# Expert rows scaled out of PSUM and added to the tokens' rows in memory by the scatters

## What is computed

```python
x = x + _L0_gnn_ref(_layernorm(x), ...)
x = x + _L0_ffn_ref(_layernorm(x), gate_w, gate_b, w1, w2, w3)
x = x + _L1_gnn_ref(_layernorm(x), ...)
...
probs = softmax(x @ gate_w + gate_b)          # 16 experts
top_probs, top_idx = top_k(probs, 2)          # two experts for each token
top_probs = top_probs / sum(top_probs)        # the gate weights
hidden = silu(x @ w1[e]) * (x @ w2[e])        # 256 -> 512, for the two experts e
out = sum over the two e of top_prob[e] * (hidden @ w3[e])
```

## Times and profile before

| | before |
|---|---|
| runs (3) | 2224.04, 2223.59, 2216.57 us |
| median | 2223.59 us |
| the profiled execution | 2217.96 us |
| its span, first to last instruction | 2215.9 us |
| mean granted TensorE clock | 0.762 |
| PE busy | 1600.6 us (72%) |
| DVE busy | 1663.4 us (75%) |
| ACT busy | 1051.1 us (47%) |
| POOL busy | 1259.5 us (57%) |

### The profile page before, as it was taken

One profiled execution on the slowest core, in us unless ns is written; L12 is line 12 of the kernel. 1 busy time (PEld: TensorE's weight loads), 2 busy tenths in 40 slices (PEclk: granted clock), 3 DMA queues, 4 the chain that ended last, 5 costly groups with the idle time before them and its releaser, 6 DMA issues. The chain is left out here.

```text
span 2215.9 us, 33302 instructions
## 1 busy us (share of the span) xinstructions
PE 1600.6 (72%) x9301; PEld 1139.8 (51%) x9301; DVE 1663.4 (75%) x4230; ACT 1051.1 (47%) x2994; POOL 1259.5 (57%) x1217
## 2 busy tenths in 40 slices
PE   0477677776767766389999994477777777777198
PEld 0477344444544445289999993333333333334176
DVE  8998777777888767587878836688888888887601
ACT  0276254444444424212222224588888888874231
POOL 0288577777777750135666650277777777760042
PEclk9888776667575655599999996776777666768589
DMA  3012465455554452388999985277777777770432
GB/s 114 1 5 10 117 190 134 133 133 134 134 133 133 130 88 69 108 275 274 307 300 305 305 277 164 99 213 208 209 209 209 210 208 204 212 175 4 108 90 24
DMA packets 212758, 352.00 MB, mean 159 GB/s; under 512 B 45840, under 2 KB 123980, under 8 KB 212588
## 3 DMA queue, kind: packets, MB, share of 16 engines
q0 software_dynamic: 75616, 167.60, 30.2%
q1 hardware_dynamic: 136972, 182.41, 26.3%
HBM read 318.55 MB, written 31.34 MB: 158 GB/s over the span
## 5 line engine op out<-in xcount | busy, mean ns | idle before, releaser
L1173 POOL DMA_INDIRECT e_rows<-table,e_gidx x880 | 845.2, 960 | 268.1 <-issue 247.6
L1233 DVE TENSOR_TENSOR acc<-acc,e_psO 128x260 f32 (+1 forms) x880 | 461.6, 525 | 61.0 <-PE e_psO L1440 23.5
L1440 PE MATMUL e_psO<-e_rows,e_oh 128*128 128x260 f32 x880 | 384.1, 594 | 133.7 <-DVE acc L1233 133.4
L1440 PEld LDWEIGHTS e_psO<-e_rows,e_oh 128*128 128x128 f32 x880 | 229.8, 287 | 229.2 <-DVE acc L1233 107.5
L2273 PE MATMUL e_psO<-e_rows,e_oh 128*128 128x456 bf16 x440 | 210.9, 479 | 71.9 <-DVE acc L1233 69.9
L798 POOL DMA_INDIRECT records<-ordered,s_chunk x68 | 119.0, 1749 | 110.8 <-DVE s_chunk L625 80.9
L1410 ACT ACTIVATE e_rows<-e_psA 128x16 f32<-128x16 f32 x110 | 20.1, 183 | 309.5 <-DVE e_psA L1401 309.5
L2178 ACT ACTIVATE away<-iota_b,etype 128x200 bf16<-128x200 bf16 x440 | 165.2, 446 | 0.0
L2274 PE MATMUL e_psO<-e_rows,e_oh 128*128 128x256 bf16 x440 | 156.3, 355 | 0.0
L2275 PE MATMUL e_psO<-e_rows,e_oh 128*128 128x256 bf16 x440 | 156.2, 355 | 0.0
L1322 PEld LDWEIGHTS e_psA<-e_own_of_unit,e_ohT 128*128 128x128 bf16 x880 | 64.2, 105 | 174.9 <-ACT e_ohT L1275 96.7
(11 more groups left out here) (443 smaller groups left out, 3689.0 us busy)
## 6 DMA issues: line engine op xcount, KB each, us to landing
hot_run<-in_L_ffn_w_dram SPq DMA_DIRECT2D x107, 512.0 KB
XN<-in_L_ffn_w_dram SPq DMA_DIRECT2D x85, 512.0 KB
e_edge_row<-edge_rows SPq DMA_DIRECT2D x110, 256.0 KB, 4.0
e_edge_row<-edge_rows SPq DMA_DIRECT2D x110, 128.0 KB, 3.2
e_rows<-table,e_gidx POOLq DMA_INDIRECT x880
table<-frow SPq DMA_DIRECT2D x25, 192.5 KB, 2.3
table<-chunk_steps SPq DMA_DIRECT2D x25, 130.0 KB, 2.1
normed_rows<-Z SPq DMA_DIRECT2D x5, 642.5 KB
```

Of the source, the lines that this page charges most:

```text
L1173: pool.indirect_dma_start(out=rows[:, r, t, 0:width], out_offset=None, in_=table, in_offset=bass.IndirectOffsetOnAxis(ap=gidx[:, r, t:t + ...
L1233: v.tensor_tensor(d, d, psO[:, units * (r % (4 // units)) + j, 0:accw], ALU.add).then_inc(S["added"], 1)
L1440: return pe.matmul(out[:, 0:A0], oh[:, r, t, :], rows[:, r, t, :], start=start, stop=stop)
```

## The change

- slot_row gets a third plane: row of the choice (its number in the list of all choices), used to look up its weight. The plane that says where to write now holds the token's own row, or a spare row for an empty slot.
- In the gate stage POOL stores X to a new tensor mixed_rows as each of five chunks of it is final.
- At the start of the expert stage TensorE turns wts, ScalarE keeps it, and POOL stores it to weight_rows in memory and waits until it has landed.
- POOL fetches the 128 weights of each tile by an indirect DMA (4 bytes to a partition), one tile further on than the current step.
- ScalarE's copy of psY scales each row by its weight, and waits for the weights.
- POOL's scatter adds to mixed_rows in memory (compute_op add), and scatter t is issued only when scatter t - 1 has landed, as a token's two choices can be in different tiles.
- In the mixing stage X is loaded from mixed_rows, five loads of 640 KB. The mixing instructions on VectorE are gone, and the copy to loops moves from ScalarE to VectorE (after L2055).

```diff
-    slot_row = sb("slot_row", [P, 2, MT], I32)
+    slot_row = sb("slot_row", [P, 3, MT], I32)
...
+                    for i in range(NCH):
+                        pool.wait_ge(pooled, i + 1)
+                        pool.dma_start(mixed_d[(1 + i * CH) * P:(1 + (i + 1) * CH) * P, :]
+                                       .rearrange("(t p) d -> p t d", p=P), X[:, i * CH:(i + 1) * CH, :])\
+                            .then_inc(mid_stored, 16)
+                    pool.wait_ge(mid_stored, 16 * NCH)
...
+                    v.tensor_copy(slot_row[:, 2, :], holder[:, 0, :])
...
+                def fetch_weight(pool, t):
+
+                    if t >= DEPTH:
+                        pool.wait_ge(weighed[t % DEPTH], t // DEPTH * 16)
+                    pool.indirect_dma_start(
+                        out=weight_of_slot[:, t:t + 1], out_offset=None, in_=weight_d,
+                        in_offset=bass.IndirectOffsetOnAxis(ap=slot_row[:, 2, t:t + 1], axis=0))\
+                        .then_inc(weighed[t % DEPTH], 16)
...
                             if s == 0:
                                 nc.gpsimd.memset(ordered1, 0.0).then_inc(cleared, 1)
+                                pool.wait_ge(wts_kept, 1)
+                                pool.dma_start(weight_d[P:(2 * NT + 1) * P, :].rearrange("(c p) w -> c (p w)", p=P),
+                                               wtsT[:, :]).then_inc(wts_stored, 16)
+                                pool.wait_ge(wts_stored, 16)
+                                fetch_weight(pool, 0)
+                            if 0 <= s < MT - 1:
+                                fetch_weight(pool, s + 1)
                             if s >= 2:
                                 t = s - 2
                                 pool.wait_ge(S["y_copied"], t + 1)
+                                if t >= 1:
+                                    pool.wait_ge(ystored[(t - 1) % DEPTH], (t - 1) // DEPTH * 16 + 16)
                                 pool.indirect_dma_start(
-                                    out=chosen_d,
+                                    out=mixed_d,
                                     out_offset=bass.IndirectOffsetOnAxis(ap=slot_row[:, 1, t:t + 1], axis=0),
-                                    in_=ys[:, t % DEPTH, :], in_offset=None).then_inc(ystored[t % DEPTH], 16)
+                                    in_=ys[:, t % DEPTH, :], in_offset=None, compute_op=ALU.add)\
+                                    .then_inc(ystored[t % DEPTH], 16)
...
-                                nc.scalar.activation(ys[:, t % DEPTH, :], psY[t % 2][:, 0:D], ACT.Copy)\
-                                    .then_inc(S["y_copied"], 1)
+                                act.wait_ge(weighed[t % DEPTH], t // DEPTH * 16 + 16)
+                                nc.scalar.activation(ys[:, t % DEPTH, :], psY[t % 2][:, 0:D], ACT.Copy,
+                                                     scale=weight_of_slot[:, t:t + 1]).then_inc(S["y_copied"], 1)
...
-                            for j in range(2):
-                                at = (1 + j * NT + i * CH) * P
-                                sp.dma_start(token_rows[j][:, i * CH:(i + 1) * CH, :],
-                                             chosen_d[at:at + CH * P, :].rearrange("(t p) d -> p t d", p=P))\
-                                    .then_inc(token_land[i], 16)
+                            at = (1 + i * CH) * P
+                            sp.dma_start(X[:, i * CH:(i + 1) * CH, :],
+                                         mixed_d[at:at + CH * P, :].rearrange("(t p) d -> p t d", p=P))\
+                                .then_inc(token_land[i], 16)
...
-                        def mix(t, j):
-
-                            xt, row = (m[:, t, :] for m in (X, token_rows[j]))
-                            v.scalar_tensor_tensor(xt, row, wts[:, j, t:t + 1], xt, ALU.mult, ALU.add).then_inc(mixed, 1)
-
...
+                            v.tensor_copy(loops[:, t, 0:D], dn.xT[:, r, :, :].rearrange("p j n -> p (j n)"))\
+                                .then_inc(turned_kept, 1)
...
-
-                                nc.scalar.activation(loops[:, bass.ds(t, 1), 0:D].rearrange("p a n -> p (a n)"),
-                                                     dn.xT[:, r, :, :].rearrange("p j n -> p (j n)"), ACT.Copy)\
-                                    .then_inc(turned_kept, 1)
```

More of the change, by code:

```diff
@@ L1696, in _ @@
                     link(v.tensor_tensor(holder[:, 1, :], holder[:, 1, :], spare_row[:, :], ALU.mult))
-                    link(v.tensor_tensor(slot_row[:, 1, :], holder[:, 1, :], holder[:, 0, :], ALU.add))
+                    link(v.tensor_tensor(slot_row[:, 1, :], holder[:, 1, :], slot_row[:, 0, :], ALU.add))
                 @block.scalar
@@ L1790, in build @@
                 cleared, chain = sem("m_cleared"), sem("m_chain")
+                weight_of_slot = sb("weight_of_slot", [P, MT], c=cc)
+                wtsT = sb("weights_turned", [2 * NT, P], c=cc)
+                wts_turned, wts_kept, wts_stored = (sem("m_wts_" + n) for n in ("turned", "kept", "stored"))
+                weighed = [sem(f"m_weighed{r}") for r in range(DEPTH)]
+                def fetch_weight(pool, t):
[5 more added lines that the diff above has]
+                        .then_inc(weighed[t % DEPTH], 16)
                 es1.start_signals()
@@ L2007, in _ @@
                         sp.wait_ge(wl_loaded, 32)
-                    @block.gpsimd
-                    def _(pool):
-                        for i in range(NCH):
-                            pool.wait_ge(token_land[i], 32)
-                            pool.sem_inc(token_have, 1)
                     @block.vector
```

29 lines of the change are left out of this document (13 added, 16 removed).

## The result

The changed kernel takes 2293.1 us (median of six runs, 2287.4 to 2300.2) where the kernel before takes 2223.1 us beside it. The forecast was 2270 us. The profiled execution took 2293.49 us, its span is 2291.8 us, 75.9 us longer than before.

The account below looks back on a forecast made before the run. TensorE paced the expert stage and VectorE the mixing stage; POOL's issuing would become the expert stage's bound. Issuing 46, wait 22 and start 2 make +70; 2218 + 70 - 18 = 2270 us, range 2236 to 2312.

Parts of the forecast that it names:

- (1): Expert stage: the scatter becomes an accumulating one, +0.56 us on POOL for each of 64.
- (2): Expert stage: each tile's fetch of 128 gate weights costs POOL 1.31 us with its gap, bounds 0 and 1.83.
- Rival B: Expert stage: POOL stays below TensorE, so 6.02 us a tile is kept; 2203 to 2208 us, chance 0.06.
- Issuing, both together: Expert stage: POOL's issuing takes 20.7 us in three tiles against TensorE's 18.04; 46 us over 17 blocks.
- (3): Expert stage: each scatter waits for the previous landing, taken as 5.5 us, lengthening the third interval; 22 us.
- The path of the wait: Expert stage: behind the wait queue records scatters, next gather and fetch, then ScalarE (four y buffers), then TensorE; no separate size.
- (4): Expert stage's start: POOL stores the weights and waits for them; 2 us, between 0 and 5.
- (5): Expert stage: DMA engines need 6.6 to 7.0 us a tile, below POOL's 7.3; they would bound if POOL did not.
- (6): Expert stage, TensorE's clock: pauses under 2.7 us, any half-rate loss swallowed by 4 us of slack; nothing added.
- The mixing stage: After the expert stage: VectorE's net -16 us and a halved first-load wait, -1.8, make -18, range -22 to -8.
- held by VectorE: Mixing stage: VectorE, busy 59.8 of 89 us, and its exchange with ScalarE for each tile hold the stage.
- Rival D: Mixing stage: ScalarE and TensorE hold its pace, so only 5 us come back; 2283 us, chance 0.13.

Follow-up runs that it names:

- the last experiment: Kernel after, gate weights brought by the gathers instead of fetched, records scatters 2, 1, 1, mixing-stage statistics two tiles further ahead: 2248.1 us, ratio 1.0134.
- the edit alone: Kernel before with only the change's mixing-stage edit; residual and second choice left out of what it computes: 2207.5 us against 2217.3, ratio 0.996.
- the lead: Mixing-stage statistics taken two tiles further ahead: ratio 1.0262 on the kernel after, 0.9984 on the kernel before, 0.9892 on before with the mixing-stage edit.

## Why the prediction was right or wrong

The side was right, and so was the mechanism of the expert stage, POOL's issuing with a wait on top; that of the mixing stage was wrong. The time was 23 us low, within the range. By its steps:

- **(1) Issue of the accumulating scatter.** Forecast +0.56 us each, measured 1.62 against 0.99 us in the groups, 27 us in all. Right.
- **(2) The fetch.** Forecast 1.005 us on POOL from a gather of 1 KB rows, measured 0.966 for 4 bytes a row. That the bytes of a row don't count holds, from 4 to 1024. That the cost follows the number of rows is not shown: every indirect DMA looked at has 112 or 128. Rival B fell with the 0.966. By the Trainium skill ("DMA: Bandwidth & Descriptors", "Anatomy of one DMA - SWDGE (gpsimd) path") descriptor generation is small; the trace disagrees with 0.97 us of issue for 512 bytes.
- **Issuing, both together: 46 us.** Measured 17.8 + 27 = 45. Right, and its form too, a slack of 2.9 us that is used up first.
- **(3) The wait.** This is the term that was mis-sized: 22 us forecast, 29 measured in the rounds and 37 in the whole. Landing of L1874 after, which was taken at 5.5:

```profile
DMA to landing us min/median/max: 3.8/5.4/7.6
```

The median was right (the trace tells the landing of 16 of the 64; without the wait it is 6.1 us, so 5.5 fitted this kernel and not the load as such). What failed in the rounds is the next number, "0.3 us to resume". Timeline of POOL, after, two scatters one after the other, and the landing of the first:

```profile
1229.54 1.62 POOL L1874 DMA_INDIRECT mixed_rows<-ln_xT,slot_row  x1 [0.30 <-issue]
...
1236.53 1.62 POOL L1874 DMA_INDIRECT mixed_rows<-ln_xT,slot_row  x1 [2.83 <-DMA mixed_rows<-ln_xT,slot_row]
...
DMA to landing us min/median/max: 6.2/6.2/6.2
```

The second starts 0.8 us after the first has landed (1236.53 - 1229.54 - 6.2), and the other scatters that wait do the same (0.77 or 0.88 us wherever the trace tells the landing). Each of the 16 intervals without records scatters holds a wait. They last 6.17 us on the mean, 1.71 more than the 4.46 us that POOL has to issue in them, where I forecast 1.3; landings of 5.4 us and 0.77 to resume give just that. The 32 longer intervals, which I had covering a landing of up to 7.9 us, cover one of 7.4 by the same account, and 8 of them hold a short wait, 3.6 us together (of the 24 waits the view puts 17 down to the landing, one to ScalarE's copy and six to "issue"). A second part I left out altogether: at the stage's end no gather, fetch or records scatter is left between the scatters, and four of them queue one landing apart. Timeline of POOL, after:

```profile
1390.85 1.00 POOL L1808 DMA_INDIRECT weight_of_slot<-weight_rows,slot_row  x1 [0.30 <-issue]
1395.10 1.57 POOL L1874 DMA_INDIRECT mixed_rows<-ln_xT,slot_row  x1 [3.25 <-DMA mixed_rows<-ln_xT,slot_row]
1399.50 1.69 POOL L1874 DMA_INDIRECT mixed_rows<-ln_xT,slot_row  x1 [2.83 <-DMA mixed_rows<-ln_xT,slot_row]
1404.21 1.54 POOL L1874 DMA_INDIRECT mixed_rows<-ln_xT,slot_row  x1 [3.02 <-DMA mixed_rows<-ln_xT,slot_row]
1408.74 1.54 POOL L1874 DMA_INDIRECT mixed_rows<-ln_xT,slot_row  x1 [3.00 <-DMA mixed_rows<-ln_xT,slot_row]
```

The prediction gave the tiles outside the sort work "about 2 us in all". From the last records scatter to the first load of the mixing stage the kernel after takes 7.7 us more than the kernel without the wait, and 3.7 more than before. The place of the wait in the rounds was right, and spreading the records scatters gave 20 us of it back.

- **The path of the wait.** I had it reach TensorE through ScalarE and the y buffers. It goes through the gathers, which stand behind the scatters on POOL and come too late for the transposes (52.2 us of TensorE's waits). The price is the same, since POOL is the bound either way.
- **(4) The stage's start.** 2 us forecast. POOL does wait 6.21 us for the store of the weights, but the first records scatter comes 87.0 us after the first gather, 86.9 before: hidden.
- **(5) DMA engines.** 6.6 to 7.0 us a tile forecast, measured 20.3 / 3 = 6.8, and below POOL's pace of 7.6. Right. The sentence that they would bound if POOL did not is borne out as far as the last experiment goes: busy 0.97 of 20.55 us, with the waits for landings still in it. I should have followed that sentence myself when I expected 18.7 to 19.3 of it.
- **(6) The clock.** Granted 0.96 in the steady part instead of 1.00. The round of the kernel without the wait, at 0.98, is still POOL's sum, so it cost nothing there. What I said of the pauses was wrong: they last up to 4.3 us where I expected under 2.7, and the clock fell after some of them. After the pause of 2.52 us that ended at 1075.91, in the columns of the earlier trace rows:

```profile
1077.00:1080.00 3.00, 3.00 (x16) 3.00 (x16) 0.00 (x0) 0.60 (x1) 1.17 (x1) 0.50 1.08 366
```

TensorE's busy share came out at 0.86 and not at 0.82, since its matmuls took 19.7 us a round where they took 18.1. The clock explains about half of that by an estimate of mine (a mean of 0.96 between the levels 1.00 and 0.50 is 0.08 of the round at the lower one, 0.9 us more); the rest isn't explained.
- **The mixing stage.** -18 us forecast, with VectorE's busy time as the bound; measured -8.6 (-9.8 for the edit alone). The step that failed is the first one, "held by VectorE": 59.8 of 89 us busy is not a bound, and the bracket of the root in the timeline of before, 1.82 us of waiting for VectorE with TensorE waiting behind, was there to be read. The price of each instruction was right (the copy takes 0.284 us, I took 0.3), and once the chain is opened the edit and the lead are worth 20.5 us. Rival D (5 back) was nearer than my -18.
- **The sum.** The wait was taken 15 us too low (37 against 22) and the gain in the mixing stage 9 too high (8.9 by the ratios against 18); start and issuing were 3 too high. That is 21 of the 23 us missed. Of the 15 us some 7 are in the rounds, the late resuming above all, and 8 at the end of the stage. (One rival was mis-added: B's own terms give 2202 to 2205 us, not 2203 to 2208.)

## What to carry to other kernels

Before adding indirect DMAs to a full loop, add up what GpSimd issues in one period (here 1.3 us for each with its gap, 1.8 to 1.9 for an accumulating one, whatever the bytes) and compare that sum, not its busy share, with the period; then do the same for the DMA engines, and keep both sums at hand, since the second takes over when the first is mended. A wait for a landing costs the landing and the time to resume (0.77 us here, against a gap of 0.30), less the time in which the queue has other DMAs to issue; where these take longer than most landings, only the late ones cost. It cost less when the other work of the queue was spread more evenly between the waits. Work taken from an engine is worth its time only where that engine is late in the chain: move the consumer's distance first, or with it.

## What the runs showed of the hardware

- An accumulating scatter of 128 rows of 1 KB leaves 96 packets more than a plain one (64 of them: 84720 packets against 78576 in the whole kernel), and costs the DMA engines 1.7 us for three of them, 0.6 us each.
- A fetch of 128 values of 4 bytes leaves 32 packets (77664 against 75616 for 64 of them) and costs GpSimd 0.97 us, as much as 128 KB.
- Under the load of the weights a plain scatter of these rows doesn't land sooner than an accumulating one: median 6.2 us against 6.1 in the two kernels without the wait, which differ in the addition alone. On engines with little else to do an accumulating one landed after 3.8 us.
- After a landing that it waited for, POOL starts the next scatter 0.77 us later; with nothing to wait for it leaves 0.30 us.
- Some of VectorE's smallest steps (128 x 5) took 0.3 to 0.6 us beside GpSimd arithmetic where they take 0.17, and others beside it kept their 0.17.
